# Gated-delta layer: Horner step on corner tiles, the w_down fold moved to the setup, signs folded into weights, and a new order of steps

## The reference, cut to what matters

```python
qkvz = xn @ w_qkvz.T                      # per head: q, k, v, z
q, k, v = causal_conv4(q, k, v)           # depthwise, 4 taps
g = -exp(A_log) * softplus(a + dt_bias);  beta = sigmoid(b)
q = l2norm(q) / 8;  k = l2norm(k)
for t in range(256):                      # per batch and head, state S is 64x64
    S = S * exp(g_t)
    delta = (v_t - k_t @ S) * beta_t
    S = S + outer(k_t, delta)
    o_t = q_t @ S
o = o * rsqrt(mean(o * o) + eps) * norm_weight * sigmoid(z)
attn = o @ w_out.T

h = fwht(xn * SU_ug) / 64                 # Walsh-Hadamard transform over 256
h = silu(h @ W_gate.T * s_gate) * (h @ W_up.T * s_up)
ffn = (fwht(h * SU_dp) / 64) @ W_down.T * s_dp     # transform over 1024
out = x + attn + ffn
```

## Time and profile before

| | |
|---|---|
| timed runs | 922.74, 921.90, 918.11 us; median 921.9 |
| profiled execution | 921.86 us, span 920.0 us |
| TensorE busy | 845.0 us, 92% (weight loads 607.2 us) |
| VectorE busy | 703.3 us, 76% |
| ScalarE busy | 256.0 us, 28% |
| GpSimd busy | 287.7 us, 31% |

### The profile page before, as it was taken

How to read it: one execution, slowest core, us unless ns; L and a number is a source line. 1 busy time by engine, 2 the same in 40 slices (tenths; PEclk the granted TensorE clock), 3 DMA queues, 4 the chain that set the end, 5 groups by cost and what they waited for, 6 DMA issues and landing times.

```text
span 920.0 us, 30578 instructions
## 1 busy us (share of the span) xinstructions
PE 845.0 (92%) x13354; PEld 607.2 (66%) x13354; DVE 703.3 (76%) x1248; ACT 256.0 (28%) x560; POOL 287.7 (31%) x194
## 2 busy tenths in 40 slices
PE   1887499999999999999999999999999999998685
PEld 1533267766767676767676677767777767767574
DVE  5675968888887979788887878797978888795522
ACT  2333114132332314141423223241414132331000
POOL 2019531514124242324142322423231513233110
PEclk9989699999999999999999999999999999999877
DMA  4323031131413131413213141304131231210101
GB/s 124 128 58 81 6 77 36 31 82 30 94 30 83 23 80 37 69 32 64 60 31 82 30 94 24 89 19 77 42 58 44 41 84 30 60 31 14 30 2 46
DMA packets 129157, 49.56 MB, mean 54 GB/s; under 512 B 110977, under 2 KB 120449, under 8 KB 128897
## 3 DMA queue, kind: packets, MB, share of 16 engines
q1 hardware_dynamic: 129024, 47.62, 23.8%
HBM read 39.98 MB, written 7.60 MB: 52 GB/s over the span
## 4 chain that ended last, share of the span: by engine, by line
PE 60%; DVE 17%; SPq 7%; DMA 6%; POOL 5%; issue 3%; ACT 1%; POOLq 0%; DVEq 0%; ACTq 0%
PE bank L581 17%; DVE kq L224 4%; PE bank L645 4%; PE bank L593 3%; PE bank L747 3%; SPq L512 3%; PE bank L662 3%; PE bank L749 3%; PE bank L692 3%; PE bank L602 3%; PE bank L664 3%; PE bank L730 2%; PE bank L668 2%; PE bank L719 2%; PE bank L678 2%
## 5 line engine op out<-in xcount | busy, mean ns | idle before, releaser
L581 PE MATMUL bank<-xnT,wq 128*128 128x512 f32 x512 | 261.8, 636 | 15.8 <-DVE kq L224 15.5
L224 DVE SCALAR_TENSOR_TENSOR kq<-bank,cw,kq 128x510 f32<-128x510 f32 (+2 forms) x288 | 214.6, 745 | 44.9 <-ACT kq L798 37.8
L581 PEld LDWEIGHTS bank<-xnT,wq 128*128 128x128 f32 x512 | 90.7, 195 | 98.1 <-issue 70.3
L948 POOL TENSOR_TENSOR ost<-ost,cst 128x8 f32<-128x8 f32 x32 | 52.3, 1634 | 191.7 <-DVE ost L357 191.7
L798 ACT ACTIVATE kq<-bank,cw 128x512 f32<-128x512 f32 x96 | 65.8, 685 | 143.3 <-PE bank L581 142.5
L944 POOL TENSOR_TENSOR Sd<-St,dec 128x256 f32<-128x256 f32 x32 | 19.9, 621 | 231.7 <-DVE St L345 161.4
L938 POOL TENSOR_TENSOR kqg<-kq,rows 128x1024 f32<-128x1024 f32 x32 | 75.5, 2358 | 39.0 <-DVE kq L224 39.0
L645 PE MATMUL bank<-kq 64*64 64x128 f32 x1024 | 69.0, 274 | 11.6 <-DVE kq L224 8.9
L911 POOL TENSOR_TENSOR kd<-kc,stat 128x512 f32<-128x512 f32 x32 | 33.4, 1042 | 144.1 <-DVE stat L261 144.1
L747 PE MATMUL bank<-wo,oT 128*128 128x256 f32 x256 | 70.6, 389 | 1.6 <-DVE oT L369 1.6
L270 DVE TENSOR_TENSOR ATP<-bank,gb 128x512 f32<-128x512 f32 x64 | 44.1, 689 | 30.4 <-issue 14.3
(11 more groups left out here) (132 smaller groups left out, 1449.1 us busy)
## 6 DMA issues: line engine op xcount, KB each, us to landing
rows<-decay_rows SPq DMA_DIRECT2D x64, 256.0 KB, 4.6
wq<-wqkvz_dram SPq DMA_DIRECT2D x16, 512.0 KB, 3.7
inverse_blocks<-UU SPq DMA_DIRECT2D x16, 256.0 KB, 2.0
woraw<-wout_dram SPq DMA_DIRECT2D x16, 128.0 KB, 2.2
wguT<-wgu_dram SPq DMA_DIRECT2D x8, 256.0 KB, 5.2
base_blocks<-ATP SPq DMA_DIRECT2D x128, 16.0 KB, 2.7
NT<-base_blocks SPq DMA_DIRECT2D x16, 128.0 KB, 2.1
U<-inverse_blocks SPq DMA_DIRECT2D x128, 16.0 KB, 2.0
```

The costliest lines, as they stand in the source:

```text
L224: nc.vector.scalar_tensor_tensor(out=y[:, :, t:S], in0=p[:, :, 0:S - t], scalar=cw[:, m, i // 2, 3 - t:4 - t], in1=y[:, :, t:S], op0=ALU.m ...
L581: last = nc.tensor.matmul(ring[i % 2][:], wq[:, q, kc, i // 2, :], xnT[:, kc, (i % 2) * 512:(i % 2) * 512 + 512], start=kc == 0, stop=kc = ...
L948: nc.gpsimd.tensor_tensor(ost[:, 2, :], ost[:, 1, :], k("neghalf")[:, 0:B * 2], ALU.pow).then_inc(rms_done, 1)
```

## The change

Four things change, and the order strings with them.

1. The signs. beta and the conv weights of v are stored negated (ScalarE negates the weights in the setup, and VectorE's and ScalarE's first use waits for it), so ATP comes out as minus the matrix, the base blocks come back into UU directly without the mask product of L296, and VectorE adds where it subtracted.
2. Q is written by ScalarE instead of VectorE, in three copies of 16 columns by 8 units per half, with the mask as a per-partition scale.
3. Horner step 1 multiplies only the two 32x32 diagonal corners of Q, in 32x32 tiles (four matmuls per unit where there were two); step 3 computes only the upper 32 output rows.
4. The fold runs on VectorE in the setup, on w_down itself before the 128-point transform, in the buffer of kqg, where it had run on GpSimd behind the first `kd`; w_down is loaded third in the setup, some small loads go to ScalarE's queue, and GpSimd's clears stand ahead of the rsqrt of the layer norm.

```diff
@@ inv 0, VectorE
                     if i == 0:
                         dve.wait_ge(nb_in, (m + 1) * 16)
-                        wait(dve, uu_out, m * 16)
-                        wait(dve, ut_done, m)
-                        step(tt(U, NT[:], k("blk"), ALU.mult))
                         step(nc.vector.memset(sub(U, 0, (BASE + 1, BASE)), 1.0))
@@ hz, VectorE
-                    if j == 0:
-                        nc.vector.tensor_tensor(Q[:, half(H), 0:n], p, k("below").unsqueeze(1).broadcast_to([P, HALF, n]), ALU.mult).then_inc(hz_done, 1)
-                        nc.vector.tensor_tensor(X[:, q, half(H), C - n:C], U16[:, half(H), C - n:C], p, ALU.subtract).then_inc(hz_done, 1)
+                    nc.vector.tensor_tensor(X[:, q, half(H), C - n:C], U16[:, half(H), C - n:C], p, ALU.add).then_inc(hz_done, 1)
@@ hz, ScalarE
+                def hz(m, q, j, H):
+                    act.wait_ge(hz_ready, m * 8 + H + 1)
+                    for i in range(NB - 1):
+                        cols = slice(i * BASE, i * BASE + BASE)
+                        nc.scalar.activation(Q[:, half(H), cols], split(M[H][:, 0:HALF * W3], HALF)[:, :, cols], ACT.Copy,
+                                             scale=k("below")[:, i * BASE:i * BASE + 1]).then_inc(q_done, 1)
@@ hz, TensorE
+                    elif j == 1:
+                        pe.wait_ge(q_done, m * 6 + 3 * (H + 1))
+                        if j == 1:
+                            for rs, cs in ((top, slice(0, H2)), (low, slice(H2, C))):
+                                for h in range(2):
+                                    last = nc.tensor.matmul(M[H][rs[h], i * n:i * n + n], Q[rs[h], u, cs], U16[rs[h], u, C - n:C], start=True, stop=True)
+                            continue
-                            elif j == 1:
-                                last = nc.tensor.matmul(dst, Q[hs[h], u, :], U16[hs[h], u, C - n:C], start=True, stop=True)
-                                last = nc.tensor.matmul(M[H][hs[h], i * n + n - H2:i * n + n], Q[hs[h], u, :], X[hs[h], q, u, H2:C], start=True, stop=True)
+                                last = nc.tensor.matmul(M[H][top[h], i * n + n - H2:i * n + n], Q[hs[h], u, 0:H2], X[hs[h], q, u, H2:C], start=True, stop=True)
@@ setup, VectorE
+                def butterfly(src, dst, h, t):
+                    s4, d4 = (w.rearrange("p (a t h) d -> p a t h d", t=2, h=h) for w in (src, dst))
+                    step(nc.vector.tensor_tensor(d4[:, :, t], s4[:, :, 0], s4[:, :, 1], (ALU.add, ALU.subtract)[t]))
+                def wscaled(i):
+                    step(nc.vector.tensor_tensor(wds[1][:, 4 * i:4 * i + 4], wds[0][:, 4 * i:4 * i + 4], wsd[:].unsqueeze(1).broadcast_to([P, 4, HID]), ALU.mult))
+                dve.wait_ge(wdn_in, 16)
+                dve.wait_ge(wsd_in, 16)
+                wscaled(0)
                 dve.wait_ge(sq_done, TT)
                 step(nc.vector.tensor_scalar(st[:, 0, :], st[:, 2, :], 1.0 / HID, LN_EPS, ALU.mult, ALU.add))
                 steps["var"] = count[0]
+                wscaled(1)
                 dve.wait_ge(rstd_done, 1)
...
                 for q in (1, 3):
+                    butterfly(wds[1], wds[0], 1, q // 2)
...
+                for t in range(2):
+                    butterfly(wds[0], wds[1], 2, t)
+                for t in range(2):
+                    butterfly(wds[1], wds[0], 4, t)
+                steps["fold"] = count[0]
@@ kd, GpSimd
-                    if m == 0 and H == 1:
-                        fold()
@@ setup, GpSimd
                 nc.gpsimd.memset(e0[:], 0.0).then_inc(e0_zero, 1)
+                nc.gpsimd.memset(U16[:], 0.0).then_inc(preset, 1)
...
                 pool.wait_ge(v_step, steps["var"])
                 nc.gpsimd.tensor_tensor(st[:, 3, :], st[:, 0, :], k("neghalf")[:, 0:TT], ALU.pow).then_inc(rstd_done, 1)
-                nc.gpsimd.memset(U16[:], 0.0).then_inc(preset, 1)
@@ order, SyncE
-                program({...}, """M.rload M.fload L.bout L.bin A.load L.uout L.uin L.oload""")
+                program({...}, """A.rload A.fload M.uout M.uin P.load A.bout A.oload A.bin""")
@@ order, GpSimd
-                program({...}, """P.kqg.0 P.kd.0 P.gb.0 P.root P.gb.1 P.kqg.1 A.sd.1 P.kd.1 A.sd.2 A.norm.0 A.norm.1""")
+                program({...}, """M.sd.1 A.kd.1 M.sd.2 M.norm.0 M.norm.1 P.gb.0 P.root P.gb.1 P.kqg.0 P.kqg.1 P.kd.0""")
```

More of the change, by code:

```diff
@@ L33 @@
 _at = 0
-for _name, _n in (("ident", P), ("eye", C), ("hsel", 2), ("below", W3), ("blk", BASE * BASE),
+for _name, _n in (("ident", P), ("eye", C), ("hsel", 2), ("below", W3),
                   ("had", P), ("half", UNITS), ("neghalf", UNITS), ("eyes", UNITS * C)):
@@ L152, in layer @@
         su, sd_, wsu, wsg = (vec[:, a:a + n] for a, n in ((0, KC), (KC, IT), (KC + IT, IT), (KC + 2 * IT, IT)))
-        wdT = xs
+        wds = [kqg[:, i].rearrange("p k u c -> p (k u c)").rearrange("p (i d) -> p i d", i=IT) for i in range(2)]
         names = """w_in row_in wo_in nw_in ff_in at_out nb_in uu_out ui_in proj_done tap0_done conv_step z_done E_done
[L156 to L162, removed]
@@ L179, in layer @@
         steps = {}
-        NINV = 17
+        NINV = 16
         def split(ap, n):
@@ L222, in proj @@
                     dve.wait_ge(tap0_done, m * 6 + i + 1)
+                    if m == 0 and i == 4:
+                        dve.wait_ge(cwv_done, 1)
                     for t in (1, 2, 3):
@@ L856, in oload @@
                     nc.scalar.activation(wo[:, q], woraw[:], ACT.Copy, scale=nwh[:]).then_inc(wo_done, 1)
+                act.dma_start(wsd[:], ws_dp.broadcast_to([P, HID])).then_inc(wsd_in, 16)
+                for h in range(2):
+                    for m, src in enumerate((alog, dtb)):
+                        act.dma_start(ah[hs[h], m, :], src[h:h + 1, :].broadcast_to([C, PAIRS])).then_inc(gate_in, 16)
+                for h in range(2):
+                    act.dma_start(nwh[hs[h], :], nw).then_inc(nw_in, 16)
                 for t in range(TT):
@@ L957, in _ @@
                 nc.gpsimd.memset(Q[:], 0.0).then_inc(preset, 1)
-                program({"root": root, "gb": gb, "kd": kd_p, "kqg": kqg_p, "sd": sd, "norm": norm}, """P.kqg.0 P.kd.0 P.gb.0 P.root P.gb.1 P.kqg.1 A.sd.1 P.kd.1 A.sd.2 A.norm.0 A.norm.1""")
+                pool.wait_ge(const_in, 16)
+                pool.wait_ge(v_step, steps["var"])
+                nc.gpsimd.tensor_tensor(st[:, 3, :], st[:, 0, :], k("neghalf")[:, 0:TT], ALU.pow).then_inc(rstd_done, 1)
+                program({"root": root, "gb": gb, "kd": kd_p, "kqg": kqg_p, "sd": sd, "norm": norm}, """M.sd.1 A.kd.1 M.sd.2 M.norm.0 M.norm.1 P.gb.0 P.root P.gb.1 P.kqg.0 P.kqg.1 P.kd.0""")
 def finish(nc, sem, yacc, out):
```

117 lines of the change are left out of this document (51 added, 66 removed).

## The result

| | before | after |
|---|---|---|
| timed runs, median | 920.9 us (918.1 to 922.7) | 908.3 us (902.7 to 909.5) |
| profiled execution | 921.86 us, span 920.0 | 909.18 us, span 907.4 |

A forecast was written before the change was run, and what follows sets the result against it. TensorE's issue was taken to bound the middle, chains of waits the start and end. From 921.9 us, start -17.5, fifteen periods -4.8 and end -0.5 gave 899.1 us; range 886 to 911, with 892 to 906 at 0.60.

The forecast's parts named there:

- (a): Start: with the fold off GpSimd, VectorE's inverse of pair 0 runs at its later pace, L296 goes; 13.0 us saved.
- (b): Start, SyncE: second pair's decay rows issued behind pair 0's base blocks, so the first store comes sooner; 2.0 us saved.
- (c): Start, GpSimd: gb done ahead of kd, so gb.0, which the ATP blocks wait for, starts sooner; 1.0 us saved.
- (d): Setup: clears moved ahead of the rsqrt leave VectorE's eight layer-norm scalings free; 3.3 us saved, at most 5.3.
- (e): Setup: the fold now costs VectorE time in the layer-norm chain; 1.8 us lost, with 0 and 4.8 as ends.
- these ends: Setup: the bounds -5.3 and +1.5 us around (d) and (e) together, said to include ScalarE's seven new DMA issues.
- The period: TensorE per pair: step 3 -0.80, step 1 +0.38, stall +0.10, together -0.32 us; fifteen periods -4.8 us.
- the band of 906 to 911: Rival: periods give nothing and half of (a) goes to waiting for pair 1's projections, 910 us; chance 0.12.
- Rival C: TensorE steps 1 and 3: issue price per instruction equal for 32x32 and 64x64 tiles; 936 us, chance 0.04; midway 0.03.
- ScalarE's Q: Each period: three copies, at most 1.15 us per half, hidden under TensorE; up to 0.7 shows if ScalarE is late.
- the stall ahead of step 3: Each period: step 3's first half waits for VectorE's sum of step 2; 0.1 us, +0.5 if VectorE is late.
- The end: Last stretch: L296 gone from the last pair's inverse, -0.5 us; with one period's gain, -0.8.

The follow-up runs named there:

- experiment 1: The kernel before with only the w_down fold and its scaling moved to VectorE in the setup, w_down and its scale loaded third: 909.5 us, ratio 0.989.
- experiment 12: Experiment 5's kernel with w_down's second scaling behind the layer norm's scalings and ScalarE's seven small loads back on SyncE's queue: 886.6 us, ratio 0.965.
- experiment 5: The changed kernel with Horner step 1 back on 64x64 tiles (64 instructions) and step 3 kept narrow: 889.2 us, ratio 0.967.
- experiment 6: The changed kernel with step 3 back to all 64 output rows and step 1 kept on four 32x32 corners: 917.6 us, ratio 0.997.
- experiment 7: Experiment 5's kernel with Horner step 2's 64 instructions sent three times, 128 more per pair: 950.2 us, ratio 1.036.
- experiment 9: Experiment 5's kernel with ks.2 put ahead of the next pair's inv.1 on VectorE: 905.2 us, ratio 0.983.
- Experiments 10 and 11: Each on experiment 5's kernel: GpSimd's clears back behind the rsqrt, 893.6 us; w_down's second scaling moved behind the layer norm's scalings, 889.9 us.

## Why the prediction was right in sign and 9 us off in size

- (a), the fold off GpSimd: right. 13.0 forecast; from the inverse's start to step 0 it is 13.8 less, and experiment 1 has 10.0 there for the fold alone, with L296 kept and one group still slow.
- (b) and (c), SyncE's and GpSimd's order: right. The store's 1.98 us are gone, and gb.0 gained 1.16 on the scan that makes E (69.39 - 63.98 before, 66.49 - 62.24 now), where 1.0 was forecast.
- (d) and (e), the setup: wrong, and covered by luck. They were to bring the setup forward by 1.5 us, and the first copy of xnT comes 1.4 later (21.44 for 20.00). The scalings gave 4.0 instead of 3.3 (6.71 to 2.67), and the rsqrt's hold-up was seen (1.64 to 2.61). But VectorE waits 3.19 us for w_down, which lands 10.7 us after issue and not 4.8, where 0.6 was taken; and that x lands 2.2 us later because of ScalarE's loads I had left inside "these ends" unpriced; experiment 12 priced it. The rsqrt starts at 14.89, beyond the 13 that the prediction called a sign of being wrong. That the inverse still starts 5.0 us sooner, where (b) to (e) had 4.5, is due to the gates, 3.1 us shorter in this execution. With gates like those of before, experiment 5 reaches step 0 16.6 us sooner, not 18.8.
- The period: this step failed. "in the middle only what TensorE issues counts" was read from busy time and taken as a sum of tile prices. The tile prices were right or too high: step 1 became 0.46 us shorter where I had added 0.38, step 3 gave its 0.80. By them each period should have won 1.1 to 1.2 us; it lost 0.35. The missing term is the supply of instructions: 888 per period instead of 824, in the densest place. At 3.5 us per 128 instructions, an estimate from the distances above, the region from gram.1 to projection 0 takes 368 / 128 x 3.5 = 10.1 us. The mean of 14 periods is 10.0 (8.80 to 10.95); without stalls it would be experiment 5's 8.85 less the 0.36 by which step 1 is shorter from start to start (1.49 for 1.85), 8.5. By the same rule experiment 5's region takes 304 / 128 x 3.5 = 8.3 us, less than its work, and it has no holes; experiment 6's takes 10.1 (mean 10.4) and experiment 7's, with 432 instructions, 11.8 (mean 12.1).
- So the range was met, but not for its reasons. 908.3 lies outside the 892 to 906 that had 0.60, in the band of 906 to 911 that had 0.12 for a start held up by pair 1's projections. The start was not held up; the periods were.
- Rival C had a price per instruction, with its point of decision at 26.7 ns. As a price per tile it is wrong, by 12 ns measured. As a rate over a packet, 3.44 us / 127 = 27 ns, it is close to what happens; the profile of before could not show it, since its densest 128 matmuls in the middle took 3.42 us.
- ScalarE's Q and the stall ahead of step 3: right, small. The hole of 0.55 at projection 6 stays.
- The end: 1.4 us longer where 0.8 less was forecast, and not explained by order (experiment 9). The stretch has a granted clock of 0.79 against 0.83 in the earlier trace rows, and 0.84 in experiment 5, where it is 88.1 us long. Experiments 10 and 11 have the same instructions there as experiment 5, and 91.1 and 90.9 us at 0.79, so a difference of 1.4 between two profiled executions shows nothing of the change. What decides the clock there stays open.

## What to carry to other kernels

Before splitting matmuls into smaller tiles, count instructions over the next few hundred, not only nanoseconds of one: here TensorE got no more than 128 float32 matmuls (with weight loads) in about 3.5 us, as a mean over three packets or so, and an idle time called "issue" that recurs at a distance of 127 or 128 instructions is its mark. Smaller output at the same count (step 3) was a gain of 0.8 us per pair; more instructions for less work (step 1) a loss. And before a step is moved, look at what runs under it on the other engines: ff and inv.1 were covers. Before a few microseconds of a profile are put down to a change, look at a stretch that the change does not touch: here the gates and the end differed by 3 us each between kernels that were the same in them.

## What the runs showed of the hardware that was not expected

- TensorE's instructions come in 16 KB packets over the DMA engines during the run, one for each 128 matmuls: 105, 113 and 121 packets for 13354, 14378 and 15402 matmuls. Ends of neighbouring holes lie 127 to 128 instructions and 3.36 to 4.02 us apart, and 5.27 to 5.97 us where the queues are 87% busy or more. A hole ends 2.2 to 3.1 us after a packet's transfer starts, and transfers start at least 3.2 us apart.
- A matmul instruction takes 12 ns where four 32x32 tiles are used in turn (1.56 us for 128), and 18.8 ns where two are (1.20 for 64). That the number of tiles makes the difference was not tested by itself.
- GpSimd's clears, which only write, slow eight one-input scalings on VectorE from 2.67 to 6.35 us.
- Seven small loads issued by ScalarE in the first microseconds delay SyncE's load of x from 4.5 to 6.8 or 7.0 us, and w_down's 1 MB from 7.0 to 10.5 or 10.7.
